# Perceiver layer on one core: the first chunk projected in the first stage, constants and first keys of the self attention made ahead of it

## The chip, the cores and the metric

The kernel runs on one core of a Trainium2 chip. The metric is the device time of one execution in microseconds (us). The engines are TensorE (PE, with PEld for its weight loads), VectorE (DVE), ScalarE (ACT), GpSimd (POOL) and SyncE (SP, which issues all DMAs here). They run their own instruction streams and wait for each other on semaphores.

## The reference

One layer of a Perceiver in fp32: cross attention, differential self attention and a thresholded mixture of experts, each on the layer norm of `x` and added to `x`. `x` is (8, 128, 512), the context (8, 2048, 512).

```
x = x + xattn(layernorm(x), ctx)     # 16 heads of 32, q/k/v/o with biases, softmax over 2048 keys
x = x + attn(layernorm(x))           # 16 heads of 64, causal; with Q1,Q2,K1,K2 the halves of a head:
    lam  = exp(sum(lq1*lk1)) - exp(sum(lq2*lk2)) + 0.8            # one number for each head
    O    = (softmax(Q1 K1^T / sqrt(32)) - lam * softmax(Q2 K2^T / sqrt(32))) V
    O    = O / rms(O) * rms_scale * 0.2 ;  out = O Wo^T
x = x + ffn(layernorm(x))            # 8 experts of 512x512, gates under 0.1 dropped
```

## The kernel before

It is five blocks, one after the other; a block ends when all engines have ended theirs. Matrix products of fp32 data are made as three fp32r products of a high part and a rest (`product`, lines 43 to 45), so each operand is turned by TensorE, copied by ScalarE (the high part) and subtracted by VectorE (the rest), a "unit" of 512 columns at a time.

1. `queries_and_weights`. An order of units, written by hand, in a ring of four PSUM banks: `wq` turned in four units, the normed `x` in eight (two halves of four batches), then eight query products, each followed by a transpose unit of `wk` or `wv`. `x`, `bq`, `wq`, `wk`, `wv` and the first context chunk are loaded in one burst in this order.
2. `cross_attention`. A clock of beats, eight to a slot; a slot projects one chunk of 512 context rows into four key units and four value units, and a tile of scores (four heads, 128 queries) is made in chunks beside it. In beats -8 to -1 the first chunk is turned, in beats 0 to 7 it is projected while the second is turned, and from beat 8 the third is turned while the second is projected. Scores start at beat 20. ScalarE evicts keys, values and high parts, VectorE the rests and the maxima.
3. `output_projection`. `wo` turned, `o` split, eight products, each added to `x1` by VectorE, layer norm in two halves, the normed `x` turned. GpSimd broadcasts the bias `bo` and adds it to `x1` ahead of VectorE.
4. `self_projections`. `Wq` and `Wk` turned, 16 query units, `Wv` turned, 16 key units, 16 value units. Queries and keys go to scratch in memory.
5. `differential_attention`, then `experts`. The attention has a prologue: SP loads the lambda vectors and `rms_scale`, the first queries and keys; GpSimd zeroes the key buffer `k_sb` (the keys are laid out block-diagonally), makes the mask and `expo` and broadcasts the coefficients to all partitions; TensorE turns `Wo` in eight units; ScalarE and VectorE split them and compute lambda. Then batches of eight steps: scores with the mask added by a matmul (L1254), maximum (L1394), exp (L1345), factors (L1407), multiplication by GpSimd (L1213), sum of the two softmax terms (L1417), transposes (L1267), output.

Operations of a tile have one line wherever they stand, so L43 to L45 are products, L801 transposes by `transpose_units`.

## Time and profile before

| | |
|---|---|
| Runs of the kernel | 1814.98, 1819.94, 1820.54 us, median 1819.94 |
| Profiled execution | 1817.25 us, span 1815.5 us, mean granted clock 0.974 |
| PE busy | 1700.9 us (94%) |
| DVE busy | 1208.1 us (67%) |
| ACT busy | 958.6 us (53%) |
| POOL busy | 695.8 us (38%) |
| DMA | 105.00 MB, mean 58 GB/s |

The profiled execution has its own time, a little over its span, since the span is what lies between the first and the last instruction. Busy time counts instructions that run; waits, semaphores and the issue of DMAs are not in it. A granted clock of 1.00 is TensorE's 2.4 GHz, 0.50 is 1.2 GHz.

### The profile page before, as it was taken

Reading aid. Unit: us, or ns where it says so; the run is one execution under the profiler, and the core shown is the slowest. Engines: PE = TensorE matmul, PEld = TensorE weight load, DVE = VectorE, ACT = ScalarE, POOL = GpSimd, SP = SyncE. Lnnn points to the kernel's source line nnn. Section 1 sums busy time; section 2 is a strip of 40 time slices with the busy share of each in tenths; the row PEclk is TensorE's granted clock in tenths of the full one; section 3 lists DMA queues with packets and bytes.
Section 4 is the critical chain, followed back from the end, with each engine's and each line's share of the span. In section 5 each row is a group of like instructions: output and inputs, shape, how many; then the busy total and the mean of one; then the engine's idle time right before and its main releaser. Section 6 shows DMA issues by size and latency. Waiting matters only on the chain. (4 is left out here: it accounts for less than half of the span.)

```text
span 1815.5 us, 37813 instructions
## 1 busy us (share of the span) xinstructions
PE 1700.9 (94%) x15753; PEld 1385.9 (76%) x15768; DVE 1208.1 (67%) x1631; ACT 958.6 (53%) x1470; POOL 695.8 (38%) x315
## 2 busy tenths in 40 slices
PE   6899999999999999999999998668998699879999
PEld 5688888888888888888888887656886466658886
DVE  5126888888878878878878888867323677753223
ACT  2236666666666666666666666643211677730000
POOL 0003555555555555555555553001001466632220
PEclk9999999999999999999999999789999899989998
DMA  4211111111111111111011102133551533101101
GB/s 162 75 47 39 35 34 41 31 37 40 30 37 41 29 39 42 28 38 42 28 39 42 27 16 75 37 112 127 174 163 37 149 92 94 46 25 51 65 0 46
DMA packets 104192, 105.00 MB, mean 58 GB/s; under 512 B 7263, under 2 KB 72799, under 8 KB 104044
## 3 DMA queue, kind: packets, MB, share of 16 engines
q1 hardware_dynamic: 104044, 102.83, 18.7%
q8 instruction: 117, 1.92, 0.4%
q14 instruction: 31, 0.25, 0.1%
HBM read 79.74 MB, written 23.07 MB: 57 GB/s over the span
## 5 line engine op out<-in xcount | busy, mean ns | idle before, releaser
L526 POOL TENSOR_TENSOR b_acc<-b_acc,b_s 128x1024 f32<-128x1024 f32 x168 | 459.0, 2732 | 258.0 <-ACT b_s L729 247.4
L758 DVE TENSOR_TENSOR b_s<-b_s,b_mb 128x2048 f32<-128x2048 f32 x128 | 365.4, 2856 | 3.9 <-ACT b_mb L716 3.9
L791 DVE TENSOR_TENSOR b_mx<-b_psS,b_mx 128x512 f32<-128x512 f32 x480 | 331.0, 690 | 51.4 <-PE b_psS L598 38.2
L729 ACT ACTIVATE b_s<-b_s 128x2048 f32<-128x2048 f32 x128 | 245.1, 1915 | 84.0 <-DVE b_s L758 84.0
L738 ACT ACTIVATE b_s<-b_psS 128x2048 f32<-128x2048 f32 x128 | 240.8, 1881 | 68.3 <-DVE b_mx L791 68.3
L43 PE MATMUL b_work<-wvT,cT 128*128 128x512 f32 x512 | 209.6, 409 | 0.0
L43 PE MATMUL b_work<-cT,wkT 128*128 128x512 f32 x512 | 207.5, 405 | 0.0
L45 PE MATMUL b_work<-wvT,cT 128*128 128x512 f32 x512 | 200.5, 392 | 0.0
L45 PE MATMUL b_work<-cT,wkT 128*128 128x512 f32 x512 | 200.5, 392 | 0.0
L44 PE MATMUL b_work<-cT,wkT 128*128 128x512 f32 x512 | 200.4, 392 | 0.0
L44 PE MATMUL b_work<-wvT,cT 128*128 128x512 f32 x512 | 199.8, 390 | 0.0
L521 POOL TENSOR_TENSOR b_acc<-b_s 128x1024 f32<-128x1024 f32 x28 | 67.1, 2397 | 277.5 <-PE b_psO L635 167.3
L598 PE MATMUL b_psS<-b_q,b_kT 32*128 32x128 f32 x4096 | 153.9, 288 | 13.2 <-ACT b_s L738 13.1
L688 ACT ACTIVATE b_kT<-b_work,b_bk 128x512 f32<-128x512 f32 x128 | 87.8, 686 | 143.8 <-PE b_work L45 143.8
L598 PEld LDWEIGHTS b_psS<-b_q,b_kT 32*128 32x128 f32 x4096 | 129.3, 190 | 37.9 <-issue 37.9
L781 DVE TENSOR_TENSOR cT<-b_work,cT 128x512 fp32r<-128x512 f32 x128 | 86.9, 681 | 73.6 <-ACT cT L721 73.5
L612 PE MATMUL b_psO<-b_s,v_sb 128*32 128x128 f32 x4096 | 130.8, 280 | 4.4 <-DVE b_oq L771 3.0
L1677 DVE SCALAR_TENSOR_TENSOR x<-f_ps,f_gate,x 128x512 f32<-128x512 f32 x64 | 47.9, 750 | 119.7 <-PE f_ps L45 119.3
L612 PEld LDWEIGHTS b_psO<-b_s,v_sb 128*32 128x32 f32 x4096 | 111.2, 112 | 17.1 <-issue 16.6
L43 PEld LDWEIGHTS b_work<-cT,wkT 128*128 128x128 f32 x512 | 96.5, 188 | 25.2
L43 PEld LDWEIGHTS b_work<-wvT,cT 128*128 128x128 f32 x512 | 96.1, 188 | 24.2
L45 PEld LDWEIGHTS b_work<-cT,wkT 128*128 128x128 f32 x512 | 96.6, 189 | 21.0
(224 smaller groups left out, 3056.1 us busy)
## 6 DMA issues: line engine op xcount, KB each, us to landing
cin<-in_ctx SPq DMA_DIRECT2D x64, 512.0 KB, 3.7
q_scratch<-d_st SPq DMA_DIRECT2D x32, 256.0 KB, 2.5
k_scratch<-d_st SPq DMA_DIRECT2D x32, 256.0 KB, 2.5
e_q<-q_scratch SPq DMA_DIRECT2D x16, 512.0 KB, 3.5
k_sb<-k_scratch SPq DMA_DIRECT2D x64, 128.0 KB, 3.6
experts_sb<-in_L_ffn_expert_w SPq DMA_DIRECT2D x8, 1024.0 KB, 5.4
x_sb<-in_x SPq DMA_DIRECT2D x2, 1024.0 KB, 6.9
q_scratch<-a_q SPq DMA_DIRECT2D x4, 512.0 KB, 3.2
```

Of the source, the lines that this page charges most:

```text
L43: nc.tensor.matmul(out, lhs[0], rhs[0], start=first, stop=False)
L44: nc.tensor.matmul(out, lhs[0], rhs[1], start=False, stop=False)
L45: return nc.tensor.matmul(out, lhs[1], rhs[0], start=False, stop=last)
L526: nc.gpsimd.tensor_tensor(acc[:, :, :], acc[:, :, :], s[:, buf, 2 * i:2 * i + 2, :], ALU.add).then_inc(sum_done, 1)
L598: last = nc.tensor.matmul(psS[:, j, t * P:(t + 1) * P], kT[h, at + t * P:at + (t + 1) * P], q[h, m % 3, :], start=True, stop=True)
L612: last = nc.tensor.matmul(psO[j * HD:(j + 1) * HD, 0:P], v[:, at + j * HD:at + (j + 1) * HD], s[:, n % BUFS, i, j * P:(j + 1) * P], start= ...
L688: nc.scalar.activation(kT[:, at:at + 512], bank[:, :], ACT.Identity, bias=bk[:, u:u + 1]).then_inc(k_done, 1)
L729: nc.scalar.activation(part, part, ACT.Exp, scale=SCALE).then_inc(exp_done, 1)
L738: nc.scalar.activation(s[:, n % BUFS, :, :].rearrange("p t (j q) -> p t j q", j=HG), psS[:, :, :].rearrange("p j (t q) -> p t j q", t=CHUN ...
L758: nc.vector.tensor_tensor(s[:, n % BUFS, :, :], s[:, n % BUFS, :, :], mb[:, :].rearrange("p (o n) -> p o n", o=1).broadcast_to([P, CHUNK, ...
L781: nc.vector.tensor_tensor(context_place(cT[1], p, n), two(work[BANK["T", p, n]]), f32(context_place(cT[0], p, n)), ALU.subtract).then_inc( ...
L791: nc.vector.tensor_tensor(mx[:, :, :], part, mx[:, :, :], ALU.max).then_inc(mx_done, 1)
```

## The change

The first block, now `queries_and_first_chunk`, has another order in a ring of eight banks: `wk` and the first chunk are loaded and turned first, then the chunk's keys and values are projected, with `wv`, the second chunk, `wq` and the normed `x` turned between them, and the eight query products come last. `x` is loaded into parts of the key buffer `b_kT` that are still free, and normed in place. Keys, values and queries are all evicted by ScalarE; the semaphores that count them are shared with the second block, which starts at beat 8.

`output_projection` takes over lambda, `rms_scale`, the mask, `expo` and the two bf16 constants. Lambda is computed for one head per partition and spread to all partitions by a matmul with ones instead of GpSimd's broadcast. `self_projections` takes over the eight units of `Wo`, between keys and values, the zeroing of the key buffer and the loads of batch 0's queries and keys. The buffers of the self attention lie where the weights were (`SelfBuffers`). `differential_attention` starts with batch 0 at once, and the loads of the first two experts stand behind the last scores.

```diff
-        self.q_out = [sem(f"q_out{i}") for i in range(2)]
+        self.q_out = [sem(f"q_out{i}") for i in range(4)]
+        self.hi_done = sem("b_hi_done")
+        self.split_done = sem("b_split_done")
+        self.k_done = sem("b_k_done")
+        self.v_done = sem("b_v_done")
...
+        order = ([("w", 0, k) for k in range(KD)] + [("c", 0, n) for n in range(4)]
+                 + [("k", 0, 0), ("w", 1, 0), ("w", 1, 1), ("k", 0, 1), ("w", 1, 2), ("w", 1, 3),
+                    ("k", 0, 2), ("c", 1, 0), ("c", 1, 1), ("k", 0, 3), ("v", 0, 0), ("c", 1, 2), ("c", 1, 3),
+                    ("v", 0, 1), ("w", 2, 0), ("w", 2, 1), ("x", 0, 0), ("x", 0, 1), ("v", 0, 2),
+                    ("w", 2, 2), ("w", 2, 3), ("x", 0, 2), ("x", 0, 3), ("v", 0, 3),
+                    ("q", 0, 0), ("x", 1, 0), ("x", 1, 1), ("q", 0, 1), ("x", 1, 2), ("x", 1, 3),
+                    ("q", 0, 2), ("q", 0, 3)] + [("q", 1, g) for g in range(G)])
...
+        parts = kT[:, :].rearrange("p (g c d) -> p g c d", g=G, c=4)
+        xs = [parts[:, t // 2, 1 + t % 2, :] for t in range(B)]
...
+            def load_context(p, h):
+                sp.dma_start(cin[:, h, :, :], ctx_in[0, (2 * p + h) * 2 * P:(2 * p + h + 1) * 2 * P, :]
+                             .rearrange("(o p) d -> p o d", p=P)).then_inc(cin_in[h], 16)
+
+            def load_weights(i):
+                sp.dma_start(w_sb[i], weights[i][0].rearrange("(o p) d -> p o d", p=P)).then_inc(w_in[i], 16)
+
+            load_weights(0)
+            for h in range(2):
+                load_context(0, h)
+            load_weights(1)
             with nc.allow_non_contiguous_dma(reason="512 numbers"):
+                sp.dma_start(bk[:, :], w["bk"].rearrange("(g p) -> p g", p=P)).then_inc(b_in, 16)
                 sp.dma_start(bq[:, :], w["bq"].rearrange("(g p) -> p g", p=P)).then_inc(b_in, 16)
-            for i in (2, 0, 1):
-                sp.dma_start(w_sb[i], weights[i][0].rearrange("(o p) d -> p o d", p=P)).then_inc(w_in[i], 16)
-            for c in range(2):
-                sp.dma_start(cin[:, c, :, :], ctx_in[0, c * 2 * P:(c + 1) * 2 * P, :]
-                             .rearrange("(o p) d -> p o d", p=P)).then_inc(shared.cin_in[c], 16)
             for g in range(G):
-                sp.wait_ge(lo_done, place["q", g, 1] + 1)
-                sp.dma_start(q_d[g].rearrange("b p t -> p b t"),
-                             q_st[:, g % 2, :].rearrange("p (b t) -> p b t", b=B)).then_inc(q_out[g % 2], 16)
+                sp.dma_start(parts[:, g, 1:3, :], x[2 * g:2 * g + 2].rearrange("b p d -> p b d")).then_inc(x_in[g // 2], 16)
+            load_weights(2)
+            for p in range(2):
+                for h in range(2):
+                    sp.wait_ge(full, place["c", p, 2 * h + 1] + 1)
+                    load_context(p + 1, h)
+            for n, (_, half, g) in enumerate(order_of["q"]):
+                sp.wait_ge(q_done, n + 1)
+                sp.dma_start(q_d[g, 4 * half:4 * half + 4].rearrange("b p t -> p b t"),
+                             q_st[:, n % 4, :].rearrange("p (b t) -> p b t", b=4)).then_inc(q_out[n % 4], 16)
...
+            for u, (kind, i, j) in enumerate(order):
+                if (kind, i, j) == ("k", 0, 0):
+                    act.wait_ge(b_in, 32)
+                if (kind, i, j) == ("c", 1, 2):
+                    norm.scalar(act)
+                act.wait_ge(full, u + 1)
+                out = bank[u % RING]
+                if kind == "w":
+                    nc.scalar.activation(weights[i][1][0][:, j, :], out[:, :], ACT.Copy).then_inc(w_hi, 1)
+                elif kind == "c":
+                    nc.scalar.activation(context_place(cT[0], i, j), two(out), ACT.Copy).then_inc(shared.hi_done, 1)
+                elif kind == "x":
+                    nc.scalar.activation(xT[0][:, j, i * 512:(i + 1) * 512], out[:, :], ACT.Copy).then_inc(x_hi, 1)
+                elif kind == "k":
+                    at = key_place(0, j, 0)
+                    nc.scalar.activation(kT[:, at:at + 512], out[:, :], ACT.Identity,
+                                         bias=bk[:, j:j + 1]).then_inc(shared.k_done, 1)
+                elif kind == "v":
+                    nc.scalar.activation(v[:, j * D:(j + 1) * D], out[:, :], ACT.Copy).then_inc(shared.v_done, 1)
+                else:
+                    n = order_of["q"].index((kind, i, j))
+                    if n >= 4:
+
+                        act.wait_ge(q_out[n % 4], 16)
+                    nc.scalar.activation(q_st[:, n % 4, :], out[:, :], ACT.Identity,
+                                         bias=bq[:, j:j + 1]).then_inc(q_done, 1)
...
+            def statistics(half):
+                dve.wait_ge(x_in[half], 32)
+                for t in range(4 * half, 4 * half + 4):
+                    norm.stats_of(xs[t], t)
+
+            def applied(half):
+                for t in range(4 * half, 4 * half + 4):
+                    norm.apply(xs[t], xs[t], t).then_inc(normed, 1)
+
+            for u, (kind, i, j) in enumerate(order):
+                if (kind, i, j) == ("w", 1, 2):
+                    statistics(0)
+                elif (kind, i, j) == ("c", 1, 0):
+                    statistics(1)
+                elif (kind, i, j) == ("c", 1, 2):
+                    norm.vector(dve)
+                    norm.done(dve)
+                elif (kind, i, j) == ("w", 2, 0):
+                    applied(0)
+                elif (kind, i, j) == ("w", 2, 2):
+                    applied(1)
+                count = counted(kind, i, j)
...
-        FIRST, LAST = -SLOT, (SLOTS + 4) * SLOT + 3
+
+        FIRST, LAST = SLOT, (SLOTS + 4) * SLOT + 3
...
-            n = steps(beat, FIRST, 2, SLOTS * CHUNK)
+            n = steps(beat, -SLOT, 2, SLOTS * CHUNK)
...
+            for i, name in enumerate(("lq1", "lq2", "lk1", "lk2")):
+                sp.dma_start(lam_in_sb[:, i, :], w_next[name]).then_inc(lam_in, 16)
+            with nc.allow_non_contiguous_dma(reason="64 numbers"):
+                for i in range(2):
+                    sp.dma_start(consts.rs[64 * i:64 * i + 64, :], w_next["rms_scale"].rearrange("(d a) -> d a", a=1)
+                                 ).then_inc(lam_in, 16)
...
+            pe.wait_ge(lam_step, 5)
+            nc.tensor.matmul(psL[:, 0:HEADS], ones[:, :], lam_diag[:, :], start=True, stop=True).then_inc(lam_full, 1)
...
+                if u == KD - 1:
+                    act.wait_ge(lam_step, 2)
+                    nc.scalar.activation(lam_e[:, :], lam_s[:, :], ACT.Exp).then_inc(lam_exp, 1)
...
+            dve.wait_ge(lam_in, 16 * 6)
+            nc.vector.tensor_tensor(lam_p[:, :, :], lam_in_sb[:, 0:2, :], lam_in_sb[:, 2:4, :],
+                                    ALU.mult).then_inc(lam_step, 1)
+            dve.wait_ge(lam_step, 1)
+            nc.vector.tensor_reduce(lam_s[:, :], lam_p[:, :, :], AX.X, ALU.add).then_inc(lam_step, 1)
+            nc.vector.memset(ones[:, :], 1.0).then_inc(lam_step, 1)
             for n in range(KD):
                 lo(n)
+            dve.wait_ge(lam_exp, 1)
+            nc.vector.tensor_tensor(lam_d[:, :], lam_e[:, 1:2], lam_e[:, 0:1], ALU.subtract).then_inc(lam_step, 1)
+            dve.wait_ge(lam_step, 4)
+            nc.vector.tensor_scalar(lam_diag[:, :], ident[0:HEADS, 0:HEADS], lam_d[:, 0:1], None,
+                                    ALU.mult).then_inc(lam_step, 1)
...
+            dve.wait_ge(lam_full, 1)
+            nc.vector.memset(consts.coef[:, :, 0:1], 1.0)
+            nc.vector.tensor_scalar(consts.coef[:, :, 1], psL[:, 0:HEADS], -LAMBDA_INIT, None, ALU.add)
+            nc.vector.tensor_scalar(consts.rs[:, :], consts.rs[:, :], 1.0 - LAMBDA_INIT, None, ALU.mult)
+            dve.wait_ge(made, 2)
+            nc.vector.tensor_copy(consts.ident_b[:, :], ident[:, :])
+            nc.vector.tensor_copy(consts.mask_b[:, :, :], mask[:, :].rearrange("p (o n) -> p o n", o=1)
+                                  .broadcast_to([P, HG, P]))
...
+def load_self(sp, q2_d, k2_d, bufs, consts, b, hf):
+    sp.dma_start(f32(bufs.q2[:, hf, :, :, :]), f32(q2_d[b, hf, :, :, :, :])).then_inc(consts.qk_in[hf], 16)
+    for j in range(HG):
+        sp.dma_start(f32(bufs.k2[j * HD:(j + 1) * HD, hf, :, :, j, :]),
+                     f32(k2_d[b, hf, j * HD:(j + 1) * HD, :, :, :])).then_inc(consts.qk_in[hf], 16)
...
+            sp.wait_ge(full, U_V)
+            sp.wait_ge(zeroed, 2)
+            for hf in range(2):
+                load_self(sp, q2_d, k2_d, bufs, consts, 0, hf)
...
+            for hf, transposed in ((1, U_Q), (0, U_K)):
+                pool.wait_ge(full, transposed)
+                nc.gpsimd.memset(f32(bufs.k2[:, hf, :, :, :, :]), 0.0).then_inc(zeroed, 1)
...
+            pe.wait_ge(shared.Wo_in, 16)
+            u = transpose_units(nc, pe, bank, ident[:, :], shared.Wo, KD, u, full, done)
...
-            for hf in range(2):
-
-                sp.wait_ge(const, hf + 1)
-                load(0, hf)
-
-            sp.wait_ge(w_full, W_UNITS)
+            with sp.Fori(1, B) as b:
+                for hf in range(2):
+
+                    sp.wait_ge(s_full, b * KB + (HALF + hf * HALF - KB))
+                    load_self(sp, q2_d, k2_d, bufs, consts, b, hf)
+
+            sp.wait_ge(s_full, B * KB)
             for r in range(2):
                 sp.dma_start(shared.experts[:, r, :, :], w_next["expert_w"][r].rearrange("(k p) d -> p k d", p=P)
                              ).then_inc(shared.expert_in[r], 16)
-            with sp.Fori(1, B) as b:
-                for hf in range(2):
-
-                    sp.wait_ge(s_full, b * KB + (HALF + hf * HALF - KB))
-                    load(b, hf)
...
-            for hf in range(2):
-                nc.gpsimd.memset(f32(k2[:, hf, :, :, :, :]), 0.0).then_inc(const, 1)
-            nc.gpsimd.memset(mask[:, :], 0.0).then_inc(const, 1)
-            pool.wait_ge(const, 3)
-
-            nc.gpsimd.affine_select(out=mask[:, :], in_=mask[:, :], compare_op=ALU.is_ge, fill=MASKED,
-                                    base=0, pattern=[[-1, P]], channel_multiplier=1).then_inc(const, 1)
-            nc.gpsimd.memset(expo[:, :], -0.5).then_inc(const, 1)
-            pool.wait_ge(lam_step, 5)
-            nc.gpsimd.partition_broadcast(coef[:, :, :].rearrange("p h s -> p (h s)"),
-                                          coef_row[:, :, :].rearrange("p h s -> p (h s)"), P).then_inc(coef_ready, 1)
-            pool.wait_ge(const, 5)
...
-            pe.wait_ge(shared.Wo_in, 16)
-            for k in range(KB):
-                if k >= 4:
-                    pe.wait_ge(w_lo, k - 3)
-                for o in range(KD):
-                    last = nc.tensor.transpose(psS[k % 4][:, o * P:(o + 1) * P], wn[:, o, k * P:(k + 1) * P],
-                                               ident[:, :])
-                last.then_inc(w_full, 1)
-            pe.wait_ge(w_lo, W_UNITS)
-
-            pe.wait_ge(lam_step, 8)
```

## Rows read from the trace of the kernel before

**Rows 1.** Windows: busy time of each engine, granted clock, DMA share, GB/s.

```profile
core 0: us, PE busy (x) PEld busy (x) DVE busy (x) ACT busy (x) POOL busy (x), PEclk, DMA share, GB/s
...
20.00:22.00 2.00, 1.47 (x10) 1.12 (x11) 2.00 (x4) 0.77 (x2) 0.00 (x0) 1.00 0.01 4
...
24.80:50.30 25.50, 25.50 (x128) 21.15 (x128) 10.28 (x15) 4.19 (x7) 0.00 (x0) 1.00 0.22 63
...
62.00:64.00 2.00, 2.00 (x6) 1.56 (x5) 0.18 (x1) 0.00 (x0) 0.00 (x0) 0.50 0.00 0
...
120.00:1250.00 1130.00, 1088.41 (x12846) 901.67 (x12844) 900.54 (x950) 723.99 (x699) 537.09 (x205) 0.98 0.13 39
```

**Rows 2.** TensorE's waits, first 100 us: total, times, longest.

```profile
PE b_work L563 <- DVE cT L781: 3.1, 1, 3.1
...
PE b_work L563 <- POOL b_ones L512: 1.8, 1, 1.8
PE a_ps L43 <- DVE a_xT L315: 1.8, 1, 1.8
```

**Rows 3.** Timeline, first block and second block's beat 8: start, us, what.

```profile
0.73 1.28 ACT L180 ACT_TABLE_LOAD   x1 [0.73 <-PEq L1719]
...
12.86 3.58 PE L258 MATMUL a_ps<-ident,w_sb 128*128 128x128 f32 x16 [12.86 <-DMA w_sb<-in_L_xattn_wq]
...
85.44 0.60 PE L563 MATMUL b_work<-ident,cin 128*128 128x128 f32 x4
```

**Rows 4.** The tile x_sb: ns min/median/max, first and last start; landings.

```profile
L184 DVE TENSOR_SCALAR a_xn<-x_sb,a_norm_mv,a_norm_rstd x8: 534/538/546, 13.7 to 19.3; 128x512 f32<-128x512 f32 x8
L230 SPq DMA_DIRECT2D x_sb<-in_x x2: 463/478/492, 0.7 to 1.2; - x2
...
DMA to landing us min/median/max: 5.8/6.9/7.9
```

**Rows 5.** Timeline, output projection.

```profile
1207.58 2.58 DVE L911 TENSOR_TENSOR c_woT<-c_ps,c_woT 128x512 fp32r<-128x512 f32 x4 [2.09 <-ACT c_woT L900]
1207.87 0.40 SPq L850 DMA_DIRECT2D wn<-in_L_attn_Wq  x1
...
1211.60 0.77 PE L43 MATMUL c_ps<-c_woT,c_oT 128*128 128x512 f32 x1 [2.80 <-issue]
...
1236.13 0.39 PE L45 MATMUL c_ps<-c_woT,c_oT 128*128 128x512 f32 x1
...
1239.45 0.67 DVE L923 TENSOR_TENSOR x<-c_ps,x 128x512 f32<-128x512 f32 x1
```

**Rows 6.** Timeline, end of the self projections to the first turned attention tile.

```profile
1394.75 0.40 PE L45 MATMUL d_ps<-d_wT,x1T 128*128 128x512 f32 x1
...
1396.15 0.57 SPq L1160 DMA_DIRECT2D e_lam_in<-in_L_attn_lq  x2
...
1396.20 1.94 PE L1242 MATMUL e_psS<-ident,Wo_sb 128*128 128x128 f32 x16 [1.05 <-PEq L943]
...
1397.96 0.59 SPq L1163 DMA_DIRECT2D e_rs<-in_L_attn_rms_scale  x1
...
1411.63 0.31 POOL L1197 PARTITION_BROADCAST e_coef<-e_coef_row  x1 [7.84 <-issue]
...
1411.97 0.69 DVE L1394 TENSOR_REDUCE e_top<-e_psS 128x4 f32<-128x512 f32 x1 [6.06 <-POOL e_coef L1197]
...
1414.71 0.16 DVE L1407 TENSOR_TENSOR e_cf<-e_rsum,e_coef 128x4 f32<-128x4 f32 x1
...
1420.55 2.03 POOL L1213 TENSOR_TENSOR e_sm<-e_sm,e_cf 128x512 f32<-128x512 f32 x2 [8.61 <-issue]
...
1422.93 0.69 PE L1267 MATMUL e_psA<-ident,e_at 128*128 128x128 f32 x2 [11.71 <-DVE e_at L1417]
```

**Rows 7.** DMA issues of the first 110 us: KB each, us to landing.

```profile
b_bv<-in_L_xattn_bv SPq DMA_DIRECT2D x1, 2.0 KB, 2.9
```

**Rows 8.** Timeline: the last scores, and the first use of an expert's weights.

```profile
1579.56 0.39 PE L1254 MATMUL e_psS<-e_mask_b,e_ident_b 128*128 128x512 bf16 x1
...
1612.75 1.92 ACT L1588 ACTIVATE f_ws<-experts_sb 128x2048 fp32r<-128x2048 f32 x1
```

More of the change, by code:

```diff
@@ L259, in _ @@
                                                    ident[:, :])
+                elif kind == "c":
+                    h, kk = divmod(j, 2)
+                    if kk == 0:
+                        pe.wait_ge(cin_in[h], 16 * (i + 1))
+                    for k in range(2):
+                        for o in range(2):
+                            last = nc.tensor.transpose(out[:, (2 * k + o) * P:(2 * k + o + 1) * P],
+                                                       cin[:, h, o, (2 * kk + k) * P:(2 * kk + k + 1) * P], ident[:, :])
                 elif kind == "x":
@@ L677, in _ @@
             for beat in range(FIRST, LAST):
-                if (x0 := projected(beat - 1)) is not None:
+                if beat > FIRST and (x0 := projected(beat - 1)) is not None:
                     p, u = x0
@@ L805, in transpose_units, with __init__, sb, output_projection @@
     return u
-def output_projection(nc, w, w_next, o_d, wn, shared):
+class SelfConstants:
+    def __init__(self, nc, ctx):
+        def sb(name, shape, dt=F32):
+            return ctx.enter_context(nc.sbuf_tensor(name, shape, dt))
+        self.coef = sb("e_coef", [P, HEADS, 2])
+        self.rs = sb("e_rs", [P, 1])
+        self.expo = sb("e_expo", [P, HEADS])
+        self.mask_b = sb("e_mask_b", [P, HG, P], BF16)
+        self.ident_b = sb("e_ident_b", [P, P], BF16)
+        self.qk_in = [ctx.enter_context(nc.semaphore(f"e_qk_in{i}")) for i in range(2)]
+def output_projection(nc, w, w_next, o_d, wn, consts, shared):
     with ExitStack() as ctx:
@@ L950, in self_projections @@
         ident, x1T = shared.ident, shared.x1T
-        wT = [[sb(f"d_wT{r}{i}", [P, KD, W2], F32R) for i in range(2)] for r in range(2)]
+        wT, woT = bufs.wT, bufs.woT
         st = sb("d_st", [P, 2, 2, 512], F32R)
```

293 lines of the change are left out of this document (142 added, 151 removed).

## Prediction

> **What bounds the kernel now.** I read the windows of busy time first, then TensorE's waits, then the timeline at the three places that the change touches. In the attention, from 120 to 1250 us, TensorE is busy in 1088 of 1130 us at a granted clock of 0.98 [rows 1]. Nothing in the diff touches what happens there, so microseconds saved ahead of it arrive at the end as they are, and so do those saved between it and the experts. The waits of the first 100 us show where TensorE has none of that density: it waits for evictions (3.1 and 1.8 us) and for the second block to open (1.8 us) [rows 2], and before all that it does nothing until 12.86 us [rows 3]. The second place is the start of the differential attention: TensorE ends its value projection at 1395.15 us and turns the first attention tile at 1422.93 us [rows 6]. The reader is to see there 27.8 us in which one thing after another is prepared.
>
> The sum is made against the profiled execution, 1817.25 us with a span of 1815.5 us. It lies 2.7 us below the median of the three runs shown (1819.94 us).
>
> **First stage.** Removed: the wait for three megabytes ahead of the first transpose, and the first eight beats of the second block, in which the first chunk is turned with nothing to project beside it. Mark the moment at which the second block's beat 8 starts, with the transposes of the third chunk: 85.44 us now [rows 3]. Up to there TensorE makes 28 transpose units and 16 products of 12 matmuls, before and after the change alike; only the order differs.
> After: the first load is one megabyte, as the first half of x is now: issued at 0.7, landed 5.8 us later [rows 4], so TensorE starts at 6.6. The first four transpose units take 3.58 us [rows 3], to 10.2; the chunk's four at 0.60 us [rows 3], to 12.6. Then the first keys wait for the last split, as the first queries do now, 1.8 us [rows 2]: 14.4. The window from 24.80 to 50.30 holds eight products and eight transpose units (128 matmuls), 3.19 us a pair [rows 1]; sixteen pairs are 51.0 us, the four units left 2.4: 67.8. The second block opens after 1.8 us, as now [rows 2].
> Is everything there in time? All six megabytes of the first burst are in by 20 us now (the window from 20 to 22 moves 4 GB/s [rows 1]). After the change it is the same six megabytes, the chunk and the value weights ahead of x. The second chunk is issued behind them and its first half is wanted at about 24.5 us, when three keys and the value weights' transposes are done; at the burst's rate, 6.3 MB in 20 us, it lands at about 22.5. SP passes four more issues (x in four parts, bk) before it reaches those loads, at 0.5 us each [rows 4], and they fall into the time in which the engines are busy with the burst anyway.
> One new stall I do expect. ScalarE takes its units in order, and the norm's square root stands behind the eviction of the first value unit. That unit is full at about 30.9 us, evicted at 31.7. VectorE waits for the root with the split of the second chunk's last half behind it, then that split and the first four applications. The root and five small steps, 0.2 us each (0.16 for such a one [rows 6]), two splits of 0.65 [rows 5] and four applications of 0.54 [rows 4] end at about 37.7 if a table load of 1.28 us [rows 3] falls in as well; TensorE wants the normed tiles at 35.9. That is 1.8 us, and 0.5 without the table load. I take 1.8.
> So beat 8 starts at 67.8 + 1.8 + 1.8 = 71.4, against 85.44: **14.0 us saved.** Bounds: 16 if there is no stall and none at the first keys, 10 if the first load takes as long as the second (7.9 us) and the second chunk is 2 us late. The loss to a low clock goes too (0.50 in the window from 62 to 64 us [rows 1]), since no gap of 3.1 us is left; it is inside the 14.0.
> The trace shows one table load at 0.73, ahead of the root, and the copies after it need none [rows 3]. The Trainium skill (ScalarE: Activation LUTs, section on table sets) says that copy and identity lie in every set as filler, and (ScalarE activation tables, section on table sets in the compiler and the runtime) that loads are placed per block by the greedy longest run. By that rule the load at the start of the block would be the root's set already, and the stall 0.5 us. The first page gives 2.66 us for a switch, with a drain; by that the stall would be 3.2 us. No run here shows either yet.
>
> The rest of the new first block costs nothing on the path. The statistics (eight operations on 512 columns, which take VectorE 0.65 us elsewhere [rows 5]) run while TensorE projects keys, and the weights they delay are wanted only by the values. Queries are evicted by ScalarE, one such operation against 2.6 us of products. The second block's first ScalarE work waits for the biases, some 3 us after the block opens (2.9 us to land [rows 7]); behind it queue the eviction of the third chunk, whose bank TensorE wants again only two products (5.2 us) later. If that cover were gone it would cost 1 us.
>
> **Output projection.** Six small loads are put ahead of Wq on SP. In the kernel before they take SP from 1396.15 to 1398.55, 2.4 us [rows 6]. So the last is issued at about 1209.7 and SP reaches Wq at 1210.3 instead of 1207.87 [rows 5]; Wq is wanted at 1250, which hides that. What isn't hidden: VectorE waits for these loads at the head of its block, and the four splits of wo, the twelve of o and with them all products are queued behind. The nearest landing is 2.9 us for the 512 single numbers of bv [rows 7]; these are 128 and fewer, and I take 2.5, so 1212.2. Three small operations more, 0.5 us, and the first split starts at 1212.7 instead of 1207.58 [rows 5]. ScalarE's exp stands ahead of the fourth copy and is ready in time. Two more small operations, 0.5 us, stand ahead of the o splits. The first product starts 5.7 us late, at 1217.3 instead of 1211.60.
> What of that reaches the end? The last product ends at 1236.52 now, and VectorE adds it only at 1239.45 [rows 5]: 2.9 us of slack, because the additions had waited for GpSimd's. Late products take the slack's place: 5.7 - 2.9 = 2.8 us on the path. At VectorE's end stand six small operations, five of 0.16 to 0.2 us (as the 0.16 of e_cf [rows 6]) and a cast of 512 columns, 1.1 us, and the block's end waits for them. **3.9 us lost.** Bounds: 1.1 if the loads land at once and the products catch up, 6 if they take 4.5 us.
>
> **Self projections.** Added: eight transpose units ahead of the values, at 0.60 us [rows 3] 4.8 us of TensorE; ScalarE and VectorE keep up with them, with eight banks. GpSimd's two memsets and the ten loads of the first keys and queries lie beside 45 us of value projection, and their buffers are free by then. If they weren't hidden they would cost 7 us.
>
> **Differential attention.** Removed: 32 transposes of Wo, six loads, both memsets, mask, lambda chain, and a broadcast on GpSimd. The broadcast starts at 1411.63 after 7.84 us of idle time, the first multiplication at 1420.55 after 8.61 us, though its factors were ready at 1414.87, and the view puts both down to issue, not to an engine [rows 6]: GpSimd is held up by nothing that a semaphore shows, on both sides of the broadcast. A change of its code is the likely reason, and after the change no broadcast stands in this block or right ahead of it. The Trainium skill (GPSIMD Engine Reference, Instruction dispatch) gives about 6 us for the first call of freshly loaded code. By its figure the second hold would be 6 us, and not the 8.6 us of the trace; I go by the trace.
> After: block change 1.05 us as now [rows 6]; one score unit, four matmuls of 0.22 us and the way to VectorE, 1.15; from the first maximum to the factors 1414.87 - 1411.97 = 2.9 [rows 6]; multiplication, addition and the step to TensorE 2.4, as from 1420.55 to 1422.93 [rows 6]. That is 7.5 us, with the added transposes 12.3, against 27.8: 15.5 us. The units after it run at the low clock now, since TensorE has idled 11 us; I add 0.5. **16.0 us saved.** Bounds: 13 if exp's table load (1.28) and the first waits of the ring come in full, 17.5 above.
> The first experts are no longer loaded at the block's head but behind the last scores. These start at 1579.56, and the first consumer is at 1612.75 [rows 8]: 33 us for a load of one megabyte that takes 5.8 to 7.9 [rows 4]. Hidden; without that cover 8 us.
>
> **Sum:** 14.0 - 3.9 + 16.0 = 26.1 us; 1817.25 - 26.1 = 1791.2 us.
>
> **Rivals.**
> (a) The forecast, 1791, chance 0.70; its own range is 1785 to 1797, from the bounds taken at about half each.
> (b) The first stage is bound by loads: TensorE starts only at 9 or waits for x or the second chunk, as the megabytes queue in one burst. For it: the first transposes wait 12.86 us now [rows 3]. Against it: one megabyte did land at 6.5. Saved there 8 instead of 14: 1797. Chance 0.12.
> (c) GpSimd's hold isn't the broadcast's but comes with the first multiplication of the block: then 8.6 us stay, 1800. For it: the cause isn't named by the trace. Against it: the same wait stands on both sides of the broadcast. Chance 0.08.
> (d) Better than forecast: the small loads land early, no table load, the ring runs ahead: 14 to 16, 2 lost, 17.5: 1786 or below. Chance 0.07.
> (e) The other side: the attention runs at a lower granted clock once the gaps ahead of it are gone. It decides from 26 us, 2.4% of 1088 us, that is a granted clock of 0.956 instead of 0.98 [rows 1]. For it: the stretch isn't at 1.00 now. Against it: what precedes it is 30 us of the same products as now. 1820 or more; chance 0.03.
>
> Runs of the kernel before lie between 1814.98 and 1820.54 us, so 0.3% (5.5 us) is about what a measurement tells from no change. Faster by more than that in (a) to (d): 0.96; within it 0.02 and slower 0.02, both from (e). The range takes (a), (b), (d) and most of (c), and the 2.7 us by which the median may stand above the profiled execution: 1783 to 1801.
>
> **What would show it.** First TensorE work at 6.6 us, first transposes of the third chunk at about 71; in the output projection the first product 5 to 6 us later against the block's start; from the last value product to the first turned attention tile 7 to 8 us; GpSimd's first multiplication within 0.2 us of its factors. The prediction is wrong if GpSimd's hold stays, if TensorE waits over 4 us in the first 60 us for loads, or if the attention's length isn't what it was.

## The result and the profile after

The changed kernel took 1790.89 us (median of 4 runs, 1789.97 to 1792.42) against 1818.68 us for the kernel before beside it (1814.98 to 1820.54). The ratio is 0.985, with an interval of 0.983 to 0.987. Timed a second time, it took 1795.65 us (1791.38 to 1797.98) against 1817.69, a ratio of 0.989 (0.987 to 0.991). The forecast was 1791.2, range 1783 to 1801: both medians lie in it, so 22 to 28 us were gained where 26 were forecast.

The profiled execution took 1792.42 us with a span of 1790.6: 24.9 us less span than before. The page's first part, busy time, share of the span and instructions of each engine:

```profile
span 1790.6 us, 37821 instructions
...
PE 1696.8 (95%) x15770; PEld 1385.6 (77%) x15770; DVE 1198.9 (67%) x1625; ACT 963.5 (54%) x1479; POOL 695.3 (39%) x314
```

TensorE has hardly less work: 1696.8 us busy instead of 1700.9. What went away is idle time, so marks on the way show where. First TensorE's waits in the first 110 us, which answer to [rows 2]:

```profile
PE a_ps L321 <- DMA w_sb<-in_L_xattn_wk: 6.5, 1, 6.5
PE a_ps L43 <- DVE cT L420: 2.2, 1, 2.2
PE a_ps L335 <- DVE b_kT L191: 2.0, 1, 2.0
PE b_work L665 <- POOL b_ones L614: 1.7, 1, 1.7
```

The work begins at 6.5 us instead of 12.9. A wait of 2.2 us stands ahead of the first keys and a new one of 2.0 us ahead of the transposes of `x` in place in `b_kT`. The timelines of ScalarE and VectorE show where that one comes from, and TensorE's shows the two marks:

```profile
30.38 0.60 ACT L379 ACTIVATE v_sb<-a_ps 128x512 f32<-128x512 f32 x1 [2.03 <-PE a_ps L45]
30.99 1.28 ACT L187 ACT_TABLE_LOAD   x1
32.29 0.21 ACT L187 ACTIVATE a_norm_root<-a_norm_veps 128x8 f32<-128x8 f32 x1
...
32.53 0.20 DVE L166 RECIPROCAL a_norm_rstd<-a_norm_root 128x8 f32<-128x8 f32 x1 [5.26 <-ACT a_norm_root L187]
...
36.83 1.06 PE L335 MATMUL a_ps<-ident,b_kT 128*128 128x128 f32 x8 [2.00 <-DVE b_kT L191]
...
70.45 0.65 PE L665 MATMUL b_work<-ident,cin 128*128 128x128 f32 x4 [1.70 <-POOL b_ones L614]
```

VectorE stands for 5.26 us until ScalarE has evicted the value unit, loaded a table and made the root. Beat 8 starts at 70.45, where it was 85.44 [rows 3]: 15.0 us saved. This profile is the best of its kind: in the profiles of the seven runs below whose first block is the change's own, beat 8 starts at 71.36 to 72.90, which is 12.5 to 14.1 us saved.

The output projection, as a timeline (it answers to [rows 5]):

```profile
1192.35 1.94 PE L895 MATMUL c_ps<-ident,wo_sb 128*128 128x128 f32 x16 [2.45 <-PEq L429]
...
1195.66 1.20 SPq L975 DMA_DIRECT2D e_rs<-in_L_attn_rms_scale  x2
1196.90 0.59 SPq L978 DMA_DIRECT2D wn<-in_L_attn_Wq  x1
...
1198.18 0.80 POOL L984 PARTITION_BROADCAST c_bo<-c_bo_row  x1 [99.20 <-issue]
1198.58 0.33 DVE L1053 TENSOR_TENSOR c_lam_p<-c_lam_in 16x64 f32<-16x64 f32 x1 [7.02 <-DMA e_rs<-in_L_attn_rms_scale]
...
1203.38 0.77 PE L43 MATMUL c_ps<-c_woT,c_oT 128*128 128x512 f32 x1 [9.10 <-DVE c_oT L1068]
...
1211.85 10.06 POOL L988 TENSOR_TENSOR x<-x,c_bo 128x512 f32<-128x512 f32 x8 [12.87 <-issue]
...
1213.16 0.69 DVE L1073 TENSOR_TENSOR x<-c_ps,x 128x512 f32<-128x512 f32 x1 [6.13 <-POOL x L988]
...
1220.70 1.22 DVE L171 TENSOR_TENSOR c_norm_tmp<-c_norm_tmp,c_norm_veps 128x4 f32<-128x4 f32 x1
...
1226.97 0.39 PE L45 MATMUL c_ps<-c_woT,c_oT 128*128 128x512 f32 x1
1228.16 0.67 DVE L1073 TENSOR_TENSOR x<-c_ps,x 128x512 f32<-128x512 f32 x1
```

The products start 11.0 us after the block's first TensorE work instead of 5.3 (1206.28 to 1211.60): 5.7 late, as forecast. But VectorE's first addition waits for GpSimd, not for them, and GpSimd stands for 12.87 us between its broadcast and its first addition, with "issue" as the only reason. In the kernel before it stood there for 9.40:

```profile
1206.28 2.52 PE L801 MATMUL c_ps<-ident,wo_sb 128*128 128x128 f32 x16 [2.46 <-PEq L320]
...
1211.93 0.97 POOL L856 PARTITION_BROADCAST c_bo<-c_bo_row  x1 [98.02 <-issue]
1222.30 2.54 POOL L860 TENSOR_TENSOR x<-x,c_bo 128x512 f32<-128x512 f32 x2 [9.40 <-issue]
...
1229.29 3.09 DVE L156 TENSOR_SCALAR c_norm_veps<-c_norm_mv 128x4 f32<-128x4 f32 x1
```

The block takes 47.0 us to the next one's first transposes instead of 44.15: 2.9 us lost.

GpSimd holds VectorE a second time, behind the fourth addition. The small norm steps on 128x4 numbers take 0.16 to 0.18 us where GpSimd is silent (from 1229.88 us). While it adds, one of them took 3.09 us in the kernel before, and three took 0.58, 0.76 and 1.22 us in the changed one. The last of these ends within 0.03 us of the end of GpSimd's eighth addition, at 1232.35 and at 1221.91. In ten of the eleven profiles VectorE's fifth addition starts 0.45 or 1.3 to 1.5 us after that end. So it is the end of GpSimd's additions, and not only their start, that sets the block. No run shows why the steps stretch.

The head of the self projections, in windows (busy time of each engine, granted clock, DMA share, GB/s), first before, then after:

```profile
1249.00:1255.00 6.00, 4.57 (x42) 4.60 (x43) 4.38 (x8) 4.29 (x10) 0.00 (x0) 1.00 0.49 177
```

```profile
1238.00:1244.00 6.00, 4.63 (x22) 4.66 (x23) 3.46 (x10) 2.49 (x5) 0.00 (x0) 0.50 0.61 181
```

In the same busy time TensorE does half as many matmuls, at the lower of its two levels. From the first transposes to the first product it takes 9.7 us instead of 6.9. The eight units of `Wo` take 3.4 us (from 1342.59 to the next product at 1346.00). With the 2.7 us of the head that is 6.1 of the 7.0 us by which the stage is longer; 0.9 us aren't found.

The head of the differential attention, which answers to [rows 6]:

```profile
1390.67 0.39 PE L45 MATMUL d_ps<-d_wT,x1T 128*128 128x512 f32 x1
...
1392.07 1.28 ACT L1481 ACT_TABLE_LOAD   x1 [44.77 <-PEq L1131]
...
1392.11 0.38 PE L1397 MATMUL e_psS<-e_mask_b,e_ident_b 128*128 128x512 bf16 x1 [1.05 <-PEq L1131]
...
1395.90 0.16 DVE L1519 TENSOR_TENSOR e_cf<-e_rsum,e_coef 128x4 f32<-128x4 f32 x1
...
1396.15 1.04 POOL L1368 TENSOR_TENSOR e_sm<-e_sm,e_cf 128x512 f32<-128x512 f32 x1 [94.80 <-DVE e_cf L1519]
...
1397.88 0.44 PE L1410 MATMUL e_psA<-ident,e_at 128*128 128x128 f32 x2 [1.92 <-DVE e_at L1529]
```

GpSimd starts 0.1 us after its factors are ready. The table load runs while the scores and their maximum are made. From the start of the last value matmul to the first turned tile it is 7.2 us instead of 28.2; from its end, as the forecast counts it, 6.8 instead of 27.8.

The whole account in span: first stage 15.0, attention -1.1, output projection -2.9, self projections and start of the attention 14.0, up to the experts -0.4, the rest 0.2; together 24.8, against 24.9 from the rounded spans. The cross attention's -1.1 need not be the change's doing: from beat 8 to the output projection it took 1120.84 us before and 1120.8 to 1121.9 in the ten profiles of the new first block.

### The profile page after: what moved, and what is told of

It is laid out like the page before. It is cut to its first block and busy times, and to the rows that moved or that the text cites. A ratio compares the mean times of both kernels' runs of the same rounds, so it can differ in the third digit from the quotient of the medians.

```text
span 1790.6 us, 37821 instructions
## 1 busy us (share of the span) xinstructions
PE 1696.8 (95%) x15770; PEld 1385.6 (77%) x15770; DVE 1198.9 (67%) x1625; ACT 963.5 (54%) x1479; POOL 695.3 (39%) x314
## 5 line engine op out<-in xcount | busy, mean ns | idle before, releaser
L43 PE MATMUL b_work<-wvT,cT 128*128 128x512 f32 x496 | 203.1, 409 | 0.0
L43 PE MATMUL b_work<-cT,wkT 128*128 128x512 f32 x496 | 200.3, 404 | 0.0
L45 PE MATMUL b_work<-wvT,cT 128*128 128x512 f32 x496 | 194.2, 391 | 0.0
L45 PE MATMUL b_work<-cT,wkT 128*128 128x512 f32 x496 | 193.7, 390 | 0.0
L44 PE MATMUL b_work<-wvT,cT 128*128 128x512 f32 x496 | 193.5, 390 | 0.0
L44 PE MATMUL b_work<-cT,wkT 128*128 128x512 f32 x496 | 193.5, 390 | 0.0
L700 PE MATMUL b_psS<-b_q,b_kT 32*128 32x128 f32 x4096 | 153.9, 288 | 13.4 <-ACT b_s L832 13.4
L1368 POOL TENSOR_TENSOR e_sm<-e_sm,e_cf 128x512 f32<-128x512 f32 x64 | 73.5, 1148 | 145.6 <-DVE e_cf L1519 144.9
L875 DVE TENSOR_TENSOR cT<-b_work,cT 128x512 fp32r<-128x512 f32 x120 | 81.7, 681 | 61.8 <-ACT cT L815 61.7
L43 PEld LDWEIGHTS b_work<-cT,wkT 128*128 128x128 f32 x496 | 93.0, 188 | 24.5
```

The lines of the kernel that those rows point to most:

```text
L43: nc.tensor.matmul(out, lhs[0], rhs[0], start=first, stop=False)
L44: nc.tensor.matmul(out, lhs[0], rhs[1], start=False, stop=False)
L45: return nc.tensor.matmul(out, lhs[1], rhs[0], start=False, stop=last)
L700: last = nc.tensor.matmul(psS[:, j, t * P:(t + 1) * P], kT[h, at + t * P:at + (t + 1) * P], q[h, m % 3, :], start=True, stop=True)
L875: nc.vector.tensor_tensor(context_place(cT[1], p, n), two(work[BANK["T", p, n]]), f32(context_place(cT[0], p, n)), ALU.subtract).then_inc( ...
```

## The experiments

What had to be told apart: whether the parts add up; what made the output projection longer, late products or GpSimd; whether GpSimd's stand belongs to the broadcast; whether the low clock behind the block is the change's doing.

**The first stage alone.** The kernel before with the new first block and the second block from beat 8 on; the later blocks as before.

```diff
-            queries_and_weights(nc, x, ctx_in, wx, q_d, cin, shared)
-            cross_attention(nc, x, ctx_in, wx, q_d, o_d, cin, shared)
+            kT = inner.enter_context(nc.sbuf_tensor("b_kT", [P, G * KV], F32))
+            queries_and_first_chunk(nc, x, ctx_in, wx, q_d, cin, kT, shared)
+            cross_attention(nc, x, ctx_in, wx, q_d, o_d, cin, kT, shared)
```

> The kernel before with the new first block and the second block from beat 8 on; output projection, self projections and differential attention as before. Theory (the parts add up, each where it stands): beat 8 starts at 70.5 us instead of 85.4, and all 15 us arrive at the end: about 1803 us, ratio 0.9915 to 0.992. Rival (the first stage's gain was partly given by, or is lost to, the later stages): the gain differs from 15 by over 2 us.

1805.71 us (1800.66 to 1807.47), ratio 0.992 with an interval of 0.989 to 0.994: 13 us by the medians, 11 to 20 by the interval, about half of the gain. The other half lies in the later blocks. That the parts add is borne out within these bounds and no closer: in this run's profile beat 8 starts at 72.55, 12.9 us earlier, but the span is only 10.0 us shorter. Blocks whose code is that of before took more time in this execution: the output projection 1.7 us, and the stretch from the first transposes of the self projections to their first product 1.6 us.

**Lambda behind the splits.** VectorE's lambda operations and ScalarE's exp stand behind the splits of `o`; the loads stay where they are.

```diff
+            for n in range(KD):
+                lo(n)
+            for i, (part, b0, b1, _) in enumerate(batches):
...
             dve.wait_ge(lam_in, 16 * 6)
...
-            for n in range(KD):
-                lo(n)
```

> The changed kernel, with lambda's work on VectorE and ScalarE moved behind the splits of o in the output projection; the six small loads stay ahead of Wq. Theory P (as predicted: the products start late, and that is the loss): the first product moves back from 11.0 to 5.4 us after the block's start and the block is 2.5 to 3 us shorter. Theory G (GpSimd's additions are late, because its code comes in behind the burst of Wq and Wk, which the six loads delay): the first product moves back just as far, but the block keeps its 47.0 us within 0.4 and GpSimd's first addition its 19.5.

**The weights wait.** SP issues `Wq` and `Wk` behind GpSimd's first addition.

```diff
+            sp.wait_ge(bo_ready, 2)
             for i, name in enumerate(("Wq", "Wk")):
```

> The changed kernel, with Wq and Wk issued only behind GpSimd's first addition of the bias. Theory G: without the burst GpSimd's hold behind the broadcast shrinks from 12.9 us to 7 to 8 (7.35 in the experts' block, where nothing is loaded), its first addition starts 14 to 15 us after the block's start instead of 19.5; the block gets at most 1 us shorter, because the late products then end last. Theory P: the hold stays at 9 to 13 us.

**Both edits.**

> Both edits of the two runs before. Theory G: first addition at 14 to 15 us and first product at 5.4 us after the block's start, so the block is 4 to 5.5 us shorter than in the changed kernel. Theory P: 2.5 to 3 us shorter, as with the splits alone.

They took 1791.51, 1793.03 and 1785.83 us. The block alone is surer than the times. With lambda behind the splits the products start on time (5.2 us into the block), GpSimd stands for 12.1 us, its additions start at 18.6, and the block takes 47.6 us: nothing gained, so theory P falls. With the weights waiting GpSimd stands for 7.0 us and starts its additions at 13.4 instead of 19.5 us into the block, but now the late products hold up the additions: 45.9 us, no less than the change's own order gives in other executions (45.9 to 47.0). Only both together shorten it clearly, to 41.7. GpSimd's timeline with both, and SP's loads behind it:

```profile
1200.23 0.83 POOL L985 PARTITION_BROADCAST c_bo<-c_bo_row  x1 [99.00 <-issue]
1208.42 10.07 POOL L989 TENSOR_TENSOR x<-x,c_bo 128x512 f32<-128x512 f32 x8 [7.36 <-issue]
...
1209.73 0.40 SPq L979 DMA_DIRECT2D wn<-in_L_attn_Wq  x1
```

So two chains end at the additions, and the one through GpSimd was the later. Its stand in this block is 7.0 to 7.4 us without the four megabytes, with the order of before 9.0 and 9.4, and with the change's order 10.8 to 12.9 with them under way. The 9.0 stands behind a broadcast that itself took 3.8 us instead of 0.8 to 1.0. In the kernel before and after, the first addition comes within 0.4 us of the landing of `Wk` (issued at 1208.31 and 1197.54, landed 14.0 and 14.7 us later); the runs bear out that the burst lengthens the stand, but its end isn't tied to the landing: in the run of the next edit, which leaves this block as it is, it came 3.1 us ahead of it, and in the run of the first stage alone 2.4 us behind it.

**The root earlier.** ScalarE makes the norm's root in the slot of the first value eviction.

```diff
-                if (kind, i, j) == ("c", 1, 2):
+                if (kind, i, j) == ("v", 0, 0):
                     norm.scalar(act)
```

> The changed kernel with one edit: ScalarE makes the norm's root in the order's slot of the first value eviction of the first chunk instead of behind the second chunk's key evictions. Theory A (the 2.0 us wait of the second chunk's transposes at 36.83 us is the root, 1.28 us of table load and its place behind evictions): the wait goes to under 0.5 us, the second chunk's transposes start 1.5 to 2.2 us earlier (near 34.9 us), and the third chunk's transposes start near 68.6 us instead of 70.45, which gives about 1,789 us. Rival: the variance sum itself is late (ready at 27.1 us), or the load of 1.28 us now stops the first value eviction and TensorE waits there for a bank: then the wait only moves, and the third chunk's transposes start within 0.5 us of 70.45.

The wait is gone. ScalarE and TensorE in the timeline:

```profile
28.53 1.28 ACT L187 ACT_TABLE_LOAD   x1
29.83 0.21 ACT L187 ACTIVATE a_norm_root<-a_norm_veps 128x8 f32<-128x8 f32 x1
30.55 0.60 ACT L379 ACTIVATE v_sb<-a_ps 128x512 f32<-128x512 f32 x1 [0.51 <-PE a_ps L45]
...
35.00 1.06 PE L335 MATMUL a_ps<-ident,b_kT 128*128 128x128 f32 x8
...
68.62 0.65 PE L665 MATMUL b_work<-ident,cin 128*128 128x128 f32 x4 [1.70 <-POOL b_ones L614]
```

The load falls in a gap in which ScalarE waited for the value products, and beat 8 starts 1.8 us before the earliest of the other profiles: the wait was the root's place. The wait costs more than its own 2.0 us. In five of the eight profiles that have it TensorE falls to its lower level behind it: the granted clock of the window from 36 to 48 us is 0.86, and from the transposes behind the wait to beat 8 it is 35.2 us instead of 33.6; in the two with the root earlier it is 1.00, and beat 8 starts at 68.62 and 68.89 instead of 70.45 to 72.90. The one execution took 1786.22 us, more gain than the edit explains.

**The constants earlier.** VectorE's scaled norm row and the two bf16 constants stand ahead of the eight additions, GpSimd's mask and exponent ahead of its broadcast.

```diff
+            nc.vector.tensor_copy(consts.ident_b[:, :], ident[:, :])
+            nc.vector.tensor_copy(consts.mask_b[:, :, :], mask[:, :].rearrange("p (o n) -> p o n", o=1)
+                                  .broadcast_to([P, HG, P]))
             for t in range(B):
```

> The changed kernel with one edit in the output projection: VectorE's copies of the identity and the mask and the scaled norm row stand in the idle stretch ahead of the eight additions instead of behind them, and GpSimd fills mask and exponent before its broadcast. Theory T (the gap between the last addition and the next stage's first transposes, 2.28 us against 1.68, is these operations in the tail): the gap shrinks by 0.5 to 1.2 us and the block with it, from 47.0 to about 46 us; the clock at the next stage's start stays a matter of TensorE's idle stretch, so 0.5 to 1 us in all, 1,790 us. Rival: the gap is set by the last addition and what the next stage's transposes wait for in any case, and the added GpSimd work ahead of the broadcast delays the additions by its own length (under 1 us): no gain, 1,791 to 1,792 us. For the lower clock behind the block (9.7 us before the first product against 7.0): theory clock-by-idle says it goes only where TensorE's idle stretch before it is shorter; if it stays at 9.7 with the gap at 1.68, the gap isn't its cause.

1786.56 us. The gap ahead of the self projections shrank from 2.28 to 1.75 us, but the broadcast came 0.5 us later and the block takes 47.5 us: no gain there. The time is below what either theory named, so it doesn't choose between them. The clock was at its higher level from 1240 us on, and the first product came 6.9 us after the transposes. That is not this edit's doing, since the same stretch took 6.9 us in the run with lambda behind the splits, whose gap is 2.28, and 8.6 in the run of the first stage alone, whose gap is 1.68 and whose blocks from here on are those of before. In eleven profiles it took 6.9 to 9.7 us, in no order that an edit explains, so the theory that ties the low clock to the gap falls.

**A broadcast that nobody needs.** GpSimd gets one at the head of the differential attention.

```diff
+            nc.gpsimd.memset(spare_row[:, :], 0.0).then_inc(spare_done, 1)
+            pool.wait_ge(spare_done, 1)
+            nc.gpsimd.partition_broadcast(spare[:, :], spare_row[:, :], P).then_inc(spare_done, 1)
+            pool.wait_ge(spare_done, 2)
```

> The changed kernel with one thing added: at the head of the differential attention GpSimd fills a row and broadcasts it to 128 partitions, an operation whose result nobody uses. Theory H (it is the broadcast that holds GpSimd, not the data it waits for: the engine stands still for about 7 us before the next ordinary operation, and for about as long before the broadcast itself): GpSimd's first factor multiplication starts some 12 to 18 us after the first TensorE work of the stage instead of 4 us, the first turned tile comes 6 to 13 us later, and the kernel takes 1,797 to 1,804 us. Rival (the hold in the kernel before was the wait for the lambda loads or for VectorE): the added operation costs its own length, under 1 us, hidden behind the 4 us in which the factors aren't ready, and the time stays at 1,790 to 1,792 us.

1802.39 us. GpSimd and TensorE in the timeline:

```profile
1392.39 0.12 POOL L1359 MEMSET e_spare_row<- 1x32 f32 x1 [90.68 <-POOLq L1131]
1398.13 0.31 POOL L1361 PARTITION_BROADCAST e_spare<-e_spare_row  x1 [5.62 <-DVE e_cf L1527]
1405.75 2.03 POOL L1376 TENSOR_TENSOR e_sm<-e_sm,e_cf 128x512 f32<-128x512 f32 x2 [7.31 <-issue]
...
1408.12 0.69 PE L1418 MATMUL e_psA<-ident,e_at 128*128 128x128 f32 x2 [11.82 <-DVE e_at L1537]
```

An operation of 0.31 us costs GpSimd 5.6 us ahead of it and 7.3 behind it. The view names VectorE for the first of the two, but the broadcast waits only for GpSimd's own memset; the factors merely came last before it. The first turned tile comes 15.7 us after the block's first work instead of 5.8, and this execution is 10 us longer than the change's profiled one. The stand belongs to the broadcast. It is not tied to loads: 0.8 MB of queries and keys move in the first half of the 7.3 us and nothing in the second, and behind the experts' broadcast no packet of any queue moves at all, in either kernel:

```profile
1588.11 0.28 POOL L1645 PARTITION_BROADCAST f_gb<-f_gb_row  x1 [16.34 <-issue]
1595.50 4.59 POOL L1649 TENSOR_TENSOR f_ws<-experts_sb,f_ws 128x2048 fp32r<-128x2048 f32 x1 [7.11 <-issue]
```

There it stands for 7.11 us, in the kernel before for 7.35.

**The change again, and four edits together.** The second has the root earlier, lambda behind the splits, the waiting weights and the early constants.

> The changed kernel once more, nothing edited, timed beside the next one in five rounds. It should give 1,790 to 1,793 us, 0.985 of before. Its profile shows how far one execution stands from the next: theory 'clock by chance' lets the stretch between the self projections' first transposes and their first product be 7.0 or 9.7 us (granted clock 1.00 or 0.50 in it) from one execution to the next; theory 'clock by TensorE's idle time in the tail' gives 9.7 us again, with the gap of 2.28 us ahead of it.

> The changed kernel with the four edits of the experiments before together: the norm's root in the slot of the first value eviction; lambda's work behind the splits of the attention's output; the loads of the query and key weights behind GpSimd's first addition; the norm row, the identity's and the mask's copies ahead of the eight additions, with GpSimd's mask and exponent ahead of its broadcast. If the gains add: 1.8 us from the first stage, 4.5 to 5.3 from the output projection, up to 2.7 from the clock at the self projections' start, so 1,781 to 1,785 us, and 0.979 to 0.982 of before against 0.985 for the unedited change. Rival: a gain ahead of the output projection or in it is taken back by a lower clock in the two attentions (their stretches differed by 2 us among the runs so far): 1,785 to 1,788 us.

In five rounds beside each other: 1795.65 us for the change, 1785.18 us with the edits (1782.9 to 1788.25), ratios to before 0.989 (0.987 to 0.991) and 0.983 (0.982 to 0.984), which don't overlap. The edits are worth 10 us by the medians. In the two profiles they are worth 8.5 us of span: 3.7 at beat 8 and 4.3 in the output projection, which is 8.0 of them. The change timed again missed its expected 1790 to 1793 us. The edits' median lies at the lower end of the rival's 1785 to 1788 us, just outside the other forecast; the rival's reason, a lower clock in the attentions, isn't seen in the cross attention of the profile, which took 1120.9 us. GpSimd's and VectorE's rows of the output projection with all four:

```profile
1196.13 0.94 POOL L991 PARTITION_BROADCAST c_bo<-c_bo_row  x1 [5.68 <-issue]
1204.04 10.07 POOL L995 TENSOR_TENSOR x<-x,c_bo 128x512 f32<-128x512 f32 x8 [6.97 <-issue]
...
1205.36 0.69 DVE L1078 TENSOR_TENSOR x<-c_ps,x 128x512 f32<-128x512 f32 x1 [4.65 <-POOL x L995]
```

That block takes 41.8 us, against 46.1 for the change beside it. GpSimd is still what the additions wait for. The change's own profile shows how far one execution stands from another: its first self product came 8.5 us behind the transposes, where theory had named 7.0 or 9.7, and its beat 8 started at 72.63 instead of 70.45, behind a lower clock:

```profile
36.00:48.00 12.00, 10.56 (x52) 8.99 (x53) 8.09 (x15) 4.44 (x9) 0.00 (x0) 0.86 0.00 0
```

## Why the prediction was right, and where it wasn't

**First stage, 14.0 forecast, 15.0 measured.** The start (6.6, measured 6.5) and the stall for the root (1.8, measured 2.0) held, and so did the reason for the stall, which the experiment with the earlier root shows. The first keys waited 2.2 instead of 1.8. The first eight transpose units took 5.1 us instead of 6.0, and the units behind them 53.0 instead of 53.4. The 15.0 is partly luck: the other seven profiles give 12.5 to 14.1, around the forecast. The sentence that the loss to a low clock goes with the gap of 3.1 us didn't hold: in five of eight profiles a low clock came back, behind the new wait of 2.0 us. SP needed 5.8 us to issue `x` in four parts, not 0.5 each; TensorE had no wait for it.

**The second table load came.** The sum had taken it in. It costs 1.28 us, and the root starts 0.02 us after the load ends. The Trainium skill (ScalarE activation tables, section on table sets in the compiler and the runtime) says that loads are placed by the greedy longest run. As I read it the load at the start would have been the root's already, and the stall 0.5; the trace has a second load at 30.99, so my reading doesn't hold here. The Trainium skill (ScalarE: Activation LUTs, What ACT_TABLE_LOAD costs) gives 2.66 us for a switch, with a drain; the trace shows the 1.28 of the load and no drain.

**Output projection, 3.9 forecast, 2.9 measured: near in size by luck, wrong in mechanism.** The lateness of the products was forecast to the tenth, 5.7 us, though on the way ScalarE's exp, said to be ready in time, stood for 4.60 us and held the copies of `o` with it. The step that failed is "Late products take the slack's place". The additions never waited for the products; TensorE's last matmul started 1.2 us ahead of the last addition. What was late was GpSimd's first addition, by 3.5 us (19.5 instead of 16.0 into the block). VectorE's norm steps, which last until GpSimd's additions end, gave 0.9 back (3.5 us to the fifth addition instead of 4.4), and what lies behind them took 0.2 more. The six small operations at the end widened the gap ahead of the next block by 0.6 us, where the sum had 1.1.

Why GpSimd was late is in part argued. Shown is that its stand is long with the four megabytes under way and short without them. The six small loads put these megabytes 3.0 us later against the block's start, so they may have covered more of the stand. I had written that the later `Wq` is hidden because it is wanted at 1250; its consumer was hidden, its traffic was not. But the first addition came at 16.0 and 18.5 us in the two profiles with the order of before and at 17.2 to 19.5 in the six with the change's order of loads and their burst. No run puts `Wq` and `Wk` ahead of the six small loads, which would tell. The loss itself is small beside what the block varies by: 45.9 to 47.0 us in the profiles of the change's own order here, 44.2 and 45.9 in the two with the order of before.

**Self projections, 4.8 forecast.** The eight units took 3.4, a term that was 1.4 too large: the 0.60 is the whole length of one unit alone, and eight in a row overlap, at 0.43 each. Against that stand 2.7 us of low clock at the head of the block, which I had not foreseen and which comes and goes from one execution to the next. The stage took 7.0 us more.

**Differential attention.** 15.5 us with the added units, and 0.5 for the clock, were forecast for the two stages; 14.0 were measured. The head is right: 6.8 us where 7.5 were written, GpSimd without a stand, the table load hidden, the first experts' load hidden (issued at 1556.15, used at 1588.10). That the stand comes from the broadcast was an inference; the added broadcast shows it. The Trainium skill (GPSIMD Engine Reference, Instruction dispatch) gives about 6 us for the first call of freshly loaded code. The stand measured 5.6 us ahead of the added broadcast, 7.0 to 7.4 behind a broadcast without a burst, and up to 12.9 with one beside it. None of these runs shows loaded code as such: behind the added broadcast the DMA queues of kind "instruction" moved nothing, and neither did they behind the experts'.

**The rivals.** (b) fell: TensorE had no wait for a load after 6.5 us. (c) fell, by GpSimd's row at 1396.15. (d) reached its 14 to 16 us in the first stage in the first profile, but with the table load that it excluded; its values for the later stages weren't reached. (e) fell in every profile: the cross attention took at most 1.1 us more than before, where (e) needs 26, and the granted clock from 120 us to its end is 0.98 in both kernels. Why the second comparison gave a gain 6 us smaller is open. The mean granted clock goes with the time there: 0.976 and 0.975 in the executions of 1791.38 and 1793.36 us, 0.973 in both of 1798. But only the first of them was profiled, so no stretch can be named.

The total is closer than its parts: in the profile the first stage gave 1.0 more than forecast, the output projection cost 1.0 less, the two later stages gave 2.0 less, and 1.3 were lost elsewhere.

## What to carry to other kernels

Before small loads are put ahead of a large one, ask not only when the large one is wanted but what its traffic will then lie beside. An engine that stands with "issue" as its reason, on both sides of one rare operation, is paying for that operation: test it by adding one somewhere else, and move it to where nobody waits. Where two chains end at the same wait, mending one shows nothing; mend both before the idea is dropped.

## What the runs showed of the hardware

- A GpSimd broadcast of 0.31 us was added, and the engine stood still for 5.6 us ahead of it and 7.3 behind it. Behind a broadcast it stood for 7.0 to 7.4 us without a burst of loads (with no packet in any queue 7.11 and 7.35) and for 9.0 to 12.9 with 4 MB of loads running.
- VectorE's norm steps on 128x4 numbers, 0.16 to 0.18 us each, took 0.58, 0.76 and 1.22 us, or one of them 1.59 to 3.17, while GpSimd added tiles of 128x512. In each case the last of them ended within 0.2 us of GpSimd's last addition.
- One stretch of the same code, behind 12 us in which TensorE is busy for 5.3 (1228 to 1240 us in the changed kernel's first profile), takes 6.9 to 9.7 us from one execution to the next, at a mean granted clock between 1.00 and 0.71. So marks of one profile can't settle effects under 3 us there.
- A ScalarE table load that falls between two evictions took 1.28 us; the operation behind it started 0.02 us later.
